# Second layer's self-attention: PSUM banks shared out anew, turns in a row, output copies one slot later, and the output product in two slots

## The chip, the cores and the metric

The kernel runs on one core of a Trainium2 chip. The metric is the device time of one execution in microseconds (us); a verdict compares medians of runs of the kernel before and of the changed kernel on the same chip.

## The reference

Two pre-norm decoder layers on x of shape (16, 256, 256): 16 batches of 256 tokens with 256 features. Each layer adds self-attention, cross-attention and a mixture of experts to x. The change concerns one of these six parts, the self-attention of the second layer:

```python
def _L1_attn_ref(x, Wq, bq, Wk, bk, Wv, bv, Wo, bo):
    h = NUM_HEADS                      # 16 heads of width 64
    q = _split_heads(x @ Wq + bq, h)   # Wq, Wk, Wv: (256, 1024)
    k = _split_heads(x @ Wk + bk, h)
    v = _split_heads(x @ Wv + bv, h)
    scale = 1.0 / jnp.sqrt(jnp.float32(ATTN_DIM))
    pattern = jnp.einsum('bhid,bhjd->bhij', k, q) * scale
    prob = jax.nn.softmax(pattern, axis=-2)
    out = jnp.einsum('bhis,bhid->bhsd', prob, v)
    return concat(out) @ Wo + bo
...
x = x + _L1_attn_ref(_layernorm(x, axis=-1), L1_attn_Wq, ...)
```

## The kernel before

x stays in SBUF throughout. The stage is `l1_attention`, from line 1235 on; it occupies the span from about 1895 to 2807 us. All four compute engines run a program of their own over the batches (`over_batches`: batches -1 to 2 written out, 3 to 14 in a loop, 15 and 16 written out), and meet at semaphores only. Each engine executes its instructions in the order written.

A batch has 16 heads, handled as 8 **pairs**, and is worked in 8 **slots** h = 0 to 7 (`batch`, one in each engine's block). Precision is kept by splitting operands into a high and a low part (`HIGH_LOW`): a product is three products (`split_product`, line 68).

For a pair, the steps are spread over several slots:

- `scores` (TensorE, line 1384): 12 products into `s_ps`, 2 banks of PSUM for the two heads of the pair.
- `maximum` (DVE, L1529), `exponents` (ACT, L1460, four instructions that also sum), in the same slot. `invert` (DVE, L1534) and `normalise` (GpSimd, L1504) one slot later.
- `turn` (TensorE, L1393): the probabilities of one head are transposed into the bank `pT_ps`, for the pair of three slots before (`TURN` = 3). `take_turned` (DVE, L1541) copies it to SBUF.
- `attend` (TensorE, L1404): the product with v into `o_ps`, for the pair of four slots before (`ATTEND` = 4). `take_out` makes its high part on ACT (L1482) and its low part on DVE (L1545), in the same slot.

Between these, each slot holds **pieces** from the table `order`, entries (kind, number, batch offset, slot). X: transposes of the normalised x of the next batch (L1416). C: the k and q of one pair (12 products). V: a quarter of v (6 products of 512 columns). W: half of the output product, on the batch before (24 products). A piece i is filled on TensorE into the bank `fill[i % 2]` and waits until the piece before it in that bank is drained (`prior_in_bank`). `drain` copies it out: for X (L1470, L1551) and C (L1473, L1555) a high part on ACT and then a low part on DVE; V (L1478) on ACT alone; W (L1565) on DVE alone, which adds it to x and after W1 makes the statistics of that batch (L254 to L261). At the end of slot 2 DVE also normalises x for the next batch (L1523).

The order of the work is thus set by hand: by the order of calls in each engine's `batch`, and by the table:

```python
order = [("C", 2, 0, 0), ("V", 0, 0, 0), ("C", 3, 0, 1), ("V", 1, 0, 1), ("C", 4, 0, 2), ("C", 5, 0, 2),
         ("C", 6, 0, 3), ("C", 7, 0, 3), ("W", 0, -1, 4), ("W", 1, -1, 4), ("V", 2, 0, 5), ("V", 3, 0, 5),
         ("X", 0, 1, 6), ("X", 1, 1, 6), ("C", 0, 1, 6), ("C", 1, 1, 7)]
```

The 8 banks of PSUM hold `s_ps` twice (4 banks), `pT_ps` (1), `o_ps` (1) and `fill` twice (2).

Of the kernel before, what the change touches and what calls it, by code (L numbers as in the profile page):

```python
# [1238 lines left out]
def l1_attention(nc, sh, Wq, bq, Wk, bk, Wv, bv, Wo, bo):  # L1239
# [10 lines left out]
    TURN, ATTEND = 3, 4  # L1250
    scale = DH ** -0.5
    with ExitStack() as ctx:
# [14 lines left out]
        with ExitStack() as prep, nc.Block() as block:  # L1267
# [105 lines left out]
        with nc.Block() as block:  # L1373

            @block.tensor
            def _(pe):
                def scores(b, h):
                    pe.wait_ge(drained["C"], done("C", h, b))
                    wait_past(pe, s_exp, PAIRS * b + h - 1)
                    for t in range(TPB):  # L1380
                        for i, (x, y) in enumerate(HIGH_LOW):
                            for n in range(2):
                                r = slice(DH * n, DH * (n + 1))
                                last = pe.matmul(s_ps[h % 2][:, n, t * SEQ:(t + 1) * SEQ], kqT[x][r, h, 1, t * P:(t + 1) * P],  # L1384
                                                 kqT[y][r, h, 0, :], start=i == 0, stop=i == len(HIGH_LOW) - 1)
                    last.then_inc(s_sc, 1)

                def turn(b, h, n):
                    pe.wait_ge(s_prob, PAIRS * b + h + 1)
                    wait_past(pe, s_pT, 2 * (PAIRS * b + h) + n)  # L1390
                    for j in range(TPB):
                        for t in range(TPB):
                            last = pe.transpose(pT_ps[:, j, t * P:(t + 1) * P], prob[:, h % RING, n, t, j * P:(j + 1) * P], sh.ident[:])  # L1393
                    last.then_inc(s_pTp, 1)

                def attend(b, h):
                    pe.wait_ge(s_pT, 2 * (PAIRS * b + h) + 2)
                    if h % (PAIRS // 2) == 0:
                        pe.wait_ge(drained["V"], per_batch["V"] * b + 2 * (h // (PAIRS // 2)) + 2)
                    wait_past(pe, s_olow, PAIRS * b + h)  # L1400
                    for j in range(TPB):
                        for n in range(2):
                            at = (2 * h + n) * DH
                            last = pe.matmul(o_ps[DH * n:DH * (n + 1), 0:SEQ], v[:, j, at:at + DH], pT[:, h % 2, n, j, :],  # L1404
                                             start=j == 0, stop=j == TPB - 1)
                    last.then_inc(s_op, 1)
# [28 lines left out]
                def batch(b):  # L1435
                    for h in range(PAIRS):
# [16 lines left out]
            def _(act):  # L1453
                def exponents(b, h):
# [3 lines left out]
                    for n in range(2):  # L1458
                        for t in range(TPB):
                            last = act.activation(prob[:, h % RING, n, t, :], s_ps[h % 2][:, n, t * SEQ:(t + 1) * SEQ], ACT.Exp,  # L1460
                                                  bias=ntop[:, h % RING, n, t:t + 1], accum_out=den[:, h % RING, n, t:t + 1])
# [18 lines left out]
                def take_out(b, h):  # L1480
                    act.wait_ge(s_op, PAIRS * b + h + 1)
                    act.copy(outT[0][:, h, :], o_ps[:, 0:SEQ]).then_inc(s_ohigh, 1)  # L1482

                def batch(b):
                    for h in range(PAIRS):
                        if live(b):
                            exponents(b, h)
                        for i, kind, number, ahead in pieces_of(h):
                            if live(b + ahead):
                                drain(i, kind, number, b + ahead)  # L1490
                        attending = lagging(b, h, ATTEND)
                        if attending:
                            take_out(*attending)
# [26 lines left out]
            def _(dve):  # L1520
# [6 lines left out]
                def maximum(b, h):  # L1527
                    dve.wait_ge(s_sc, PAIRS * b + h + 1)
                    dve.tensor_reduce(ntop[:, h % RING], s_ps[h % 2][:].rearrange("p n (t s) -> p n t s", t=TPB), AXIS.X, ALU.max,  # L1529
# [6 lines left out]
                def take_turned(b, h, n):  # L1536
# [1540 lines left out]
```

## Time and profile before

| | |
|---|---|
| median of 3 runs | 3611.78 us (3607.95 to 3613.28) |
| profiled execution | 3634.84 us |
| its span | 3633.1 us |
| mean granted TensorE clock | 0.885 of 2.4 GHz |
| PE busy over the span | 2888.5 us (80%) |
| DVE, ACT, POOL busy | 1816.4, 1211.6, 500.2 us |

The profile is of one execution. PE is TensorE's matmul, PEld its weight load, DVE VectorE, ACT ScalarE, POOL GpSimd. A timeline row is the start and length in us, the engine, the line, the operation, out<-in; in brackets the idle time of that engine before it and what ended it. A waits row says who waited for whom. A window row gives busy us of each engine (and its instructions), then the granted clock as a share of full speed (1.00 is 2.4 GHz, 0.50 is 1.2 GHz) and the DMA share.

### The profile page before, as it was taken

What the parts mean: (1) busy time and instruction counts of PE and PEld (TensorE: products, weight loads), DVE (VectorE), ACT (ScalarE), POOL (GpSimd) and SP (SyncE); (2) the same over time, 40 slices, a digit from 0 to 9 for tenths busy, and PEclk for the clock granted to TensorE, in tenths of its full rate; (3) what the DMA queues carried; (4) which work ended last, traced back from release to release, by engine and by line L of the source; (5) the groups of instructions that cost most, each with busy time, mean ns of one, the idle gap of its engine ahead of it and who ended that gap; (6) DMA issues with size and microseconds to landing.
All of it is one profiled execution on the core that took longest, in us unless ns stands there. A gap on an engine that the chain in (4) does not pass through costs nothing. (4 is left out here: it accounts for less than half of the span.)

```text
span 3633.1 us, 55877 instructions
## 1 busy us (share of the span) xinstructions
PE 2888.5 (80%) x17893; PEld 2222.8 (61%) x17894; DVE 1816.4 (50%) x4037; ACT 1211.6 (33%) x3124; POOL 500.2 (14%) x408
## 2 busy tenths in 40 slices
PE   4877699999853999999218889888887879965397
PEld 3765577777652776776116777777776856644263
DVE  4555477777342222222355556555555657745323
ACT  1330134334220112112234444445443446640021
POOL 0000000000014000000423222223222101100303
PEclk9988699999865999999659999999999889985696
DMA  7000000000133111110220000000000643314363
GB/s 269 0 0 2 0 1 0 0 0 0 35 116 131 32 35 32 32 34 32 68 79 1 1 0 0 0 0 0 0 0 9 196 123 88 87 56 158 114 182 121
DMA packets 165353, 184.96 MB, mean 51 GB/s; under 512 B 22208, under 2 KB 152464, under 8 KB 163728
## 3 DMA queue, kind: packets, MB, share of 16 engines
q1 hardware_dynamic: 136464, 144.86, 12.8%
q0 software_dynamic: 9216, 25.18, 2.2%
q10 hardware_dynamic: 19584, 13.79, 1.2%
q8 instruction: 49, 0.80, 0.1%
q14 instruction: 40, 0.33, 0.0%
HBM read 115.57 MB, written 68.19 MB: 51 GB/s over the span
## 5 line engine op out<-in xcount | busy, mean ns | idle before, releaser
L1504 POOL TENSOR_TENSOR a_prob<-a_prob,a_rden 128x1024 f32<-128x1024 f32 x128 | 242.4, 1894 | 681.6 <-DVE a_rden L1534 681.6
L1460 ACT ACTIVATE a_prob<-a_s_ps,a_ntop 128x256 f32<-128x256 f32 x512 | 235.6, 473 | 293.6 <-DVE a_ntop L1529 293.6
L2645 PE MATMUL e0x_up_ps<-e0w_upT,e0x_xgT 128*128 x576 | 263.9, 601 | 0.8 <-ACT e0x_xgT L2688 0.6
L2663 PE MATMUL e0x_y_ps<-e0w_downT,e0x_hT 128*128 x1152 | 260.5, 379 | 1.0 <-DVE e0x_hT L2704 1.0
L2663 PEld LDWEIGHTS e0x_y_ps<-e0w_downT,e0x_hT 128*128 128x128 f32 x1152 | 218.8, 190 | 61.3 <-issue 35.2
L2711 DVE COPY e0x_y<-e0x_y_ps 128x256 f32<-128x256 f32 x72 | 30.6, 425 | 438.7 <-PE e0x_y_ps L2663 438.7
L1555 DVE SCALAR_TENSOR_TENSOR a_kqT_low<-a_fill,a_kq_bias,a_kqT_high 128x256 fp32r<-128x256 f32 x256 | 109.2, 479 | 231.8 <-ACT a_kqT_high L1473 231.8
L1393 PE MATMUL a_pT_ps<-ident,a_prob 128*128 128x128 f32 x1024 | 168.1, 289 | 57.1 <-DVE a_pT L1541 56.5
L2065 ACT ACTIVATE x1a_prob<-x1a_st_ps,x1a_mask_now 128x512 f32<-128x512 f32 x256 | 162.3, 687 | 88.2 <-PE x1a_st_ps L1996 86.0
L2119 DVE TENSOR_REDUCE x1a_top<-x1a_s_ps 128x4 f32<-128x1024 f32 x128 | 155.9, 1222 | 70.0 <-PE x1a_s_ps L1980 68.3
L1541 DVE COPY a_pT<-a_pT_ps 128x512 f32<-128x512 f32 x256 | 172.0, 672 | 35.5 <-PE a_pT_ps L1393 35.4
L1393 PEld LDWEIGHTS a_pT_ps<-ident,a_prob 128*128 128x128 f32 x1024 | 119.0, 145 | 89.4 <-DVE a_pT L1541 50.7
L2645 PEld LDWEIGHTS e0x_up_ps<-e0w_upT,e0x_xgT 128*128 128x128 f32 x576 | 104.3, 191 | 106.6 <-issue 106.1
L2691 ACT ACTIVATE e0x_h<-e0x_up_ps 128x512 f32<-128x512 f32 x144 | 86.0, 597 | 244.2 <-PE e0x_up_ps L2645 244.2
L1529 DVE TENSOR_REDUCE a_ntop<-a_s_ps 128x4 f32<-128x1024 f32 x128 | 155.8, 1218 | 3.3 <-PE a_s_ps L1384 1.6
L1086 ACT ACTIVATE x0b_sq<-x0b_f 128x1024 f32<-128x1024 f32 x64 | 67.9, 1061 | 261.1 <-DVE x0b_f L1158 261.1
L2748 POOL DMA_INDIRECT e0c_ya<-sorted_results,e_slots x64 | 62.2, 972 | 623.1 <-PEq L2739 595.2
L1404 PE MATMUL a_o_ps<-a_pT,a_v 128*64 128x256 f32 x1024 | 146.1, 408 | 1.0 <-DVE a_outT_low L1545 1.0
L2688 ACT COPY e0x_xgT<-e0x_t_ps 128x256 f32<-128x256 f32 x72 | 26.8, 372 | 327.8 <-PE e0x_t_ps L2636 327.8
L68 PE MATMUL a_fill<-a_xT_high,a_wk_high 128*128 128x256 f32 x256 | 85.0, 332 | 54.5 <-DVE a_xT_low L1551 51.9
L1041 PE MATMUL x_bank<-x0b_b_sb,x0b_gT 128*128 128x256 f32 x512 | 118.6, 385 | 7.2 <-issue 3.7
L1473 ACT ACTIVATE a_kqT_high<-a_fill,a_kq_bias 128x256 fp32r<-128x256 f32 x256 | 104.7, 491 | 56.0 <-PE a_fill L68 56.0
(539 smaller groups left out, 7206.0 us busy)
## 6 DMA issues: line engine op xcount, KB each, us to landing
x_qk<-head_rows SPq DMA_DIRECT2D x384, 64.0 KB
head_rows<-x1p_rows_out SPq DMA_DIRECT2D x32, 512.0 KB, 4.0
e1w_ew<-in_L_ffn_expert_w_dram SPq DMA_DIRECT2D x8, 2048.0 KB, 17.9
sorted_tokens<-zeros SPq DMA_DIRECT2D x12, 1024.0 KB, 21.1
e1x_xg<-sorted_tokens SPq DMA_DIRECT2D x96, 128.0 KB, 2.3
sorted_results<-e1x_y ACTq DMA_DIRECT2D x96, 128.0 KB, 2.4
e0x_xg<-sorted_tokens SPq DMA_DIRECT2D x72, 128.0 KB, 2.0
sorted_results<-e0x_y SPq DMA_DIRECT2D x72, 128.0 KB, 1.7
```

The costliest lines, as they stand in the source:

```text
L1041: pe.matmul(o[:, t * DIM:(t + 1) * DIM], gT[:, h, t * P:(t + 1) * P], b_sb[:, h, :], start=h == 0, stop=False)
L1393: last = pe.transpose(pT_ps[:, j, t * P:(t + 1) * P], prob[:, h % RING, n, t, j * P:(j + 1) * P], sh.ident[:])
L1404: last = pe.matmul(o_ps[DH * n:DH * (n + 1), 0:SEQ], v[:, j, at:at + DH], pT[:, h % 2, n, j, :], start=j == 0, stop=j == TPB - 1)
L1460: last = act.activation(prob[:, h % RING, n, t, :], s_ps[h % 2][:, n, t * SEQ:(t + 1) * SEQ], ACT.Exp, bias=ntop[:, h % RING, n, t:t + 1], ...
L1504: last = pool.tensor_tensor(p, p, scale_of, ALU.mult)
L1529: dve.tensor_reduce(ntop[:, h % RING], s_ps[h % 2][:].rearrange("p n (t s) -> p n t s", t=TPB), AXIS.X, ALU.max, negate=True).then_inc(s_t ...
L1541: dve.tensor_copy(pT[:, h % 2, n], pT_ps[:]).then_inc(s_pT, 1)
L1555: last = dve.scalar_tensor_tensor(kqT[1][:, number, side, :], bank[:, side * SEQ:(side + 1) * SEQ], kq_bias[:, side, number:number + 1], k ...
L2065: last = act.activation(prob[:, c % 2, j, 2 * (h % 2):2 * (h % 2) + 2, :], st_ps[:, :, j * SEQ:(j + 1) * SEQ], ACT.Exp, bias=mask_now[:, p ...
L2119: dve.tensor_reduce(dst, s_ps[h % 2][:].rearrange("p n (t s) -> p n t s", t=TPB), AXIS.X, ALU.max).then_inc(s_max, 1)
L2645: last = pe.matmul(up_ps[half][:], xgT[:, p, k, :], upT[:, bass.ds(e, 1), k, half * 512:(half + 1) * 512].rearrange("p a d -> p (a d)"), s ...
L2663: last = pe.matmul(y_ps[p][:, 0:DIM], hT[:, p, c, :], downT[:, bass.ds(e, 1), c, :].rearrange("p a d -> p (a d)"), start=c == 0, stop=c == ...
```

## The change

The scores get one pair of banks in place of two, the turned probabilities two banks (one for each head) and the output two (by the parity of the pair). The waits on them follow. Both turns and both `take_turned` come before the pieces. Output copies run five slots after the scores (`TAKE` = 5), one after the attend, ahead of the drains; for the last pair of a batch at the very start of slot 4. W0 and W1 stand in slots 4 and 5, C5 in slot 3, C7 in slot 5, V2 and V3 with both X in slot 6, C0 in slot 7.

```diff
-    TURN, ATTEND = 3, 4
+    TURN, ATTEND, TAKE = 3, 4, 5
...
-        s_ps = [ps(f"s_ps{n}", [P, 2, 512]) for n in range(2)]
-        pT_ps = ps("pT_ps", [P, TPB, SEQ])
-        o_ps = ps("o_ps", [P, 512])
+        s_ps = ps("s_ps", [P, 2, 512])
+        pT_ps = [ps(f"pT_ps{n}", [P, TPB, SEQ]) for n in range(2)]
+        o_ps = [ps(f"o_ps{n}", [P, 512]) for n in range(2)]
...
-        order = [("C", 2, 0, 0), ("V", 0, 0, 0), ("C", 3, 0, 1), ("V", 1, 0, 1), ("C", 4, 0, 2), ("C", 5, 0, 2),
-                 ("C", 6, 0, 3), ("C", 7, 0, 3), ("W", 0, -1, 4), ("W", 1, -1, 4), ("V", 2, 0, 5), ("V", 3, 0, 5),
-                 ("X", 0, 1, 6), ("X", 1, 1, 6), ("C", 0, 1, 6), ("C", 1, 1, 7)]
+        order = [("C", 2, 0, 0), ("V", 0, 0, 0), ("C", 3, 0, 1), ("V", 1, 0, 1), ("C", 4, 0, 2), ("C", 5, 0, 3),
+                 ("C", 6, 0, 3), ("W", 0, -1, 4), ("C", 7, 0, 5), ("W", 1, -1, 5), ("V", 2, 0, 6), ("V", 3, 0, 6),
+                 ("X", 0, 1, 6), ("X", 1, 1, 6), ("C", 0, 1, 7), ("C", 1, 1, 7)]
...
                 def scores(b, h):
-                    wait_past(pe, s_exp, PAIRS * b + h - 1)
+                    wait_past(pe, s_exp, PAIRS * b + h)
...
                 def turn(b, h, n):
-                    wait_past(pe, s_pT, 2 * (PAIRS * b + h) + n)
+                    wait_past(pe, s_pT, 2 * (PAIRS * b + h) + n - 1)
...
                 def attend(b, h):
-                    wait_past(pe, s_olow, PAIRS * b + h)
+                    wait_past(pe, s_olow, PAIRS * b + h - 1)
...
                         if turning:
                             turn(*turning, 0)
+                            turn(*turning, 1)
                         for i, kind, number, ahead in pieces:
                             piece(i, kind, number, b + ahead, b)
-                        if turning:
-                            turn(*turning, 1)
...
                 def take_out(b, h):
                     act.wait_ge(s_op, PAIRS * b + h + 1)
-                    act.copy(outT[0][:, h, :], o_ps[:, 0:SEQ]).then_inc(s_ohigh, 1)
+                    if h == 0:
+                        wait_past(act, filled["W"], TPB * b)
+                    act.copy(outT[0][:, h, :], o_ps[h % 2][:, 0:SEQ]).then_inc(s_ohigh, 1)
...
+                        taking = lagging(b, h, TAKE)
+                        last_pair = taking and taking[1] == PAIRS - 1
+                        if last_pair:
+                            take_out(*taking)
                         if live(b):
                             exponents(b, h)
+                        if taking and not last_pair:
+                            take_out(*taking)
```

DVE's `batch` changes in the same way: output copy of the last pair, maximum, invert, both `take_turned`, output copy, drains. `maximum` and `exponents` read the one `s_ps`.

ACT in slots 5 and 6 before (batch 1; `a_v` is a V drain, `a_outT_high` the high part of an output; the semaphores carry the names of their first users, `n0_dve_step` is the attend's):

```order
L1460 ACTIVATE a_prob,a_den<-a_s_ps,a_ntop 128x256 [waits load_x0_loaded,load_zeroed]
L1460 ACTIVATE a_prob,a_den<-a_s_ps,a_ntop 128x256 x3
L1478 COPY a_v<-a_fill 128x512 [waits a0_pT_ready] x2
L1482 CAST a_outT_high<-a_o_ps 128x256 [waits n0_dve_step]
L1460 ACTIVATE a_prob,a_den<-a_s_ps,a_ntop 128x256 [waits load_x0_loaded,load_zeroed]
L1460 ACTIVATE a_prob,a_den<-a_s_ps,a_ntop 128x256 x3
L1470 CAST a_xT_high<-a_fill 128x256 [waits a0_x_updated] x2
```

and now, the same two slots:

```order
L1459 ACTIVATE a_prob,a_den<-a_s_ps,a_ntop 128x256 [waits load_x0_loaded,load_zeroed]
L1459 ACTIVATE a_prob,a_den<-a_s_ps,a_ntop 128x256 x3
L1483 CAST a_outT_high<-a_o_ps 128x256 [waits a0_pT_in_psum,n0_dve_step]
L1472 ACTIVATE a_kqT_high<-a_fill,a_kq_bias 128x256 [waits a0_out_in_psum]
L1472 ACTIVATE a_kqT_high<-a_fill,a_kq_bias 128x256
L1459 ACTIVATE a_prob,a_den<-a_s_ps,a_ntop 128x256 [waits load_x0_loaded,load_zeroed]
L1459 ACTIVATE a_prob,a_den<-a_s_ps,a_ntop 128x256 x3
L1483 CAST a_outT_high<-a_o_ps 128x256 [waits n0_dve_step]
L1477 COPY a_v<-a_fill 128x512 [waits a0_pT_ready] x2
L1469 CAST a_xT_high<-a_fill 128x256 [waits a0_x_updated] x2
```

The output copy has moved ahead of the drains, the first of a batch waits for `a0_pT_in_psum` too, which is the count of filled W pieces, and C7 and both V and X copies stand behind it.

DVE before, in slot 4 and the start of slot 5 (`x_resident<-x_resident,a_fill` adds a W piece, `a_ntop` is the maximum):

```order
L1541 COPY a_pT<-a_pT_ps 128x512
L1565 TENSOR_TENSOR x_resident<-x_resident,a_fill 128x256 x2
L55 MEMSET scratch 128x1
L254 BN_STATS a_parts<-x_resident 128x6 x2
L55 MEMSET scratch 128x1
L258 BN_AGGR a_means<-a_parts 128x2 x2
L261 TENSOR_SCALAR x_stats<-a_means 128x4
L1541 COPY a_pT<-a_pT_ps 128x512
L1545 TENSOR_TENSOR a_outT_low<-a_o_ps,a_outT_high 128x256
L1529 TENSOR_REDUCE a_ntop<-a_s_ps 128x4
```

and now, slot 5 and the start of slot 6:

```order
L1533 TENSOR_REDUCE a_ntop<-a_s_ps 128x4
L1538 RECIPROCAL a_rden<-a_den 128x4
L1545 COPY a_pT<-a_pT_ps 128x512 x2
L1549 TENSOR_TENSOR a_outT_low<-a_o_ps,a_outT_high 128x256
L1559 SCALAR_TENSOR_TENSOR a_kqT_low<-a_fill,a_kq_bias,a_kqT_high 128x256 x2
L1569 TENSOR_TENSOR x_resident<-x_resident,a_fill 128x256
L55 MEMSET scratch 128x1
L254 BN_STATS a_parts<-x_resident 128x6 x2
L55 MEMSET scratch 128x1
L258 BN_AGGR a_means<-a_parts 128x2 x2
L261 TENSOR_SCALAR x_stats<-a_means 128x4
L1533 TENSOR_REDUCE a_ntop<-a_s_ps 128x4
```

W1's addition and the statistics stood behind W0's and ahead of a turned copy; they stand behind C7's low part and directly ahead of slot 6's maximum.

TensorE now, from the last product of V3 in slot 6 to the first of C0 in slot 7 (before, `L1416 MATMUL a_fill<-ident,a_xn`, the X pieces, was followed at once by that C0 product):

```order
L68 MATMUL a_fill<-a_wv_high,a_xT_low 128x512
L1416 MATMUL a_fill<-ident,a_xn 128x128 x4
L1404 MATMUL a_o_ps<-a_pT,a_v 64x256 x4
L1384 MATMUL a_s_ps<-a_kqT_high 128x256 x2
L1384 MATMUL a_s_ps<-a_kqT_low,a_kqT_high 128x256 x2
L1384 MATMUL a_s_ps<-a_kqT_high,a_kqT_low 128x256 x2
L1384 MATMUL a_s_ps<-a_kqT_high 128x256 x2
L1384 MATMUL a_s_ps<-a_kqT_low,a_kqT_high 128x256 x2
L1384 MATMUL a_s_ps<-a_kqT_high,a_kqT_low 128x256 x2
L1393 MATMUL a_pT_ps<-ident,a_prob 128x128 x8
L68 MATMUL a_fill<-a_xT_high,a_wk_high 128x256
```

Attend, scores and two turns have come between X and C0.

## Rows read from the trace of the kernel before

**Rows 1.** Busy time by engine in batches 1 to 14: window, length, engines, clock, DMA

```profile
1950.38:2734.76 784.38, 692.25 (x5547) 566.93 (x5546) 454.81 (x966) 372.26 (x1317) 229.34 (x126) 0.96 0.00 0
```

**Rows 2.** Waits of PE, same stretch: us in total, times, longest

```profile
PE a_fill L68 <- DVE a_xT_low L1551: 47.5, 14, 3.4
PE a_pT_ps L1393 <- DVE a_pT L1541: 44.2, 54, 1.3
```

**Rows 3.** Timeline of PE: W0 to the next turn, then one C and V slot

```profile
2201.81 0.36 PE L68 MATMUL a_fill<-a_wo_high,a_outT_high 128*128 128x256 f32 x1
...
2207.56 0.60 PE L1393 MATMUL a_pT_ps<-ident,a_prob 128*128 128x128 f32 x4
...
2236.66 0.38 PE L1384 MATMUL a_s_ps<-a_kqT_high 64*128 64x256 f32 x2
...
2237.98 0.37 PE L68 MATMUL a_fill<-a_xT_high,a_wk_high 128*128 128x256 f32 x1
...
2239.50 0.39 PE L68 MATMUL a_fill<-a_wv_high,a_xT_high 128*128 128x512 f32 x1
...
2240.89 0.60 PE L1393 MATMUL a_pT_ps<-ident,a_prob 128*128 128x128 f32 x4
2241.42 1.08 PE L1404 MATMUL a_o_ps<-a_pT,a_v 128*64 128x256 f32 x8
2242.43 0.39 PE L1384 MATMUL a_s_ps<-a_kqT_high 64*128 64x256 f32 x2
```

**Rows 4.** Timeline of PE: slot 6 and the start of slot 7

```profile
2215.23 0.39 PE L1384 MATMUL a_s_ps<-a_kqT_high 64*128 64x256 f32 x2
...
2220.62 0.38 PE L68 MATMUL a_fill<-a_xT_high,a_wk_high 128*128 128x256 f32 x1 [3.39 <-DVE a_xT_low L1551]
...
2225.21 0.39 PE L1384 MATMUL a_s_ps<-a_kqT_high 64*128 64x256 f32 x2
```

**Rows 5.** Windows of one microsecond inside that slot's C piece

```profile
2222.00:2223.00 1.00, 1.00 (x7) 1.00 (x5) 0.00 (x0) 0.00 (x0) 0.00 (x0) 0.50 0.00 0
```

**Rows 6.** Timeline of ACT: V copies, a slot with one C, C copies of two

```profile
2213.72 1.08 ACT L1478 COPY a_v<-a_fill 128x512 f32<-128x512 f32 x2
...
2227.56 0.47 ACT L1460 ACTIVATE a_prob<-a_s_ps,a_ntop 128x256 f32<-128x256 f32 x1 [1.86 <-DVE a_ntop L1529]
...
2229.37 0.85 ACT L1473 ACTIVATE a_kqT_high<-a_fill,a_kq_bias 128x256 fp32r<-128x256 f32 x2
2230.08 0.40 ACT L1482 CAST a_outT_high<-a_o_ps 128x256 fp32r<-128x256 f32 x1
...
2246.60 1.58 ACT L1473 ACTIVATE a_kqT_high<-a_fill,a_kq_bias 128x256 fp32r<-128x256 f32 x4
```

**Rows 7.** Timeline of DVE: the same slot, and slot 2's normalisation

```profile
2226.22 1.22 DVE L1529 TENSOR_REDUCE a_ntop<-a_s_ps 128x4 f32<-128x1024 f32 x1
...
2230.25 0.88 DVE L1555 SCALAR_TENSOR_TENSOR a_kqT_low<-a_fill,a_kq_bias,a_kqT_high 128x256 fp32r<-128x256 f32 x2 [2.15 <-ACT a_kqT_high L1473]
2231.04 0.68 DVE L1541 COPY a_pT<-a_pT_ps 128x512 f32<-128x512 f32 x1
...
2231.97 1.22 DVE L1529 TENSOR_REDUCE a_ntop<-a_s_ps 128x4 f32<-128x1024 f32 x1
...
2249.99 0.73 DVE L1523 TENSOR_SCALAR a_xn<-x_resident,x_stats,x_rstd 128x256 f32 x2
```

**Rows 8.** Timeline of DVE: W1 added, statistics, next instruction

```profile
2263.48 0.42 DVE L1565 TENSOR_TENSOR x_resident<-x_resident,a_fill 128x256 f32 x1 [2.31 <-PE a_fill L68]
...
2265.25 0.69 DVE L1541 COPY a_pT<-a_pT_ps 128x512 f32<-128x512 f32 x1
```

**Rows 9.** First layer: waits of PE, 60 to 260 us, and two windows

```profile
PE a_wt L437 <- DVE a_xn L551: 33.9, 15, 2.6
...
129.00:131.00 2.00, 2.00 (x6) 1.55 (x6) 0.00 (x0) 0.50 (x1) 0.00 (x0) 0.50 0.00 0
179.00:181.00 2.00, 2.00 (x11) 1.77 (x10) 0.00 (x0) 0.91 (x3) 0.00 (x0) 1.00 0.00 0
```

More of the change, by code:

```diff
@@ L1383, in scores @@
                                 r = slice(DH * n, DH * (n + 1))
-                                last = pe.matmul(s_ps[h % 2][:, n, t * SEQ:(t + 1) * SEQ], kqT[x][r, h, 1, t * P:(t + 1) * P],
+                                last = pe.matmul(s_ps[:, n, t * SEQ:(t + 1) * SEQ], kqT[x][r, h, 1, t * P:(t + 1) * P],
                                                  kqT[y][r, h, 0, :], start=i == 0, stop=i == len(HIGH_LOW) - 1)
@@ L1389, in turn @@
                     pe.wait_ge(s_prob, PAIRS * b + h + 1)
-                    wait_past(pe, s_pT, 2 * (PAIRS * b + h) + n)
+                    wait_past(pe, s_pT, 2 * (PAIRS * b + h) + n - 1)
                     for j in range(TPB):
                         for t in range(TPB):
-                            last = pe.transpose(pT_ps[:, j, t * P:(t + 1) * P], prob[:, h % RING, n, t, j * P:(j + 1) * P], sh.ident[:])
+                            last = pe.transpose(pT_ps[n][:, j, t * P:(t + 1) * P], prob[:, h % RING, n, t, j * P:(j + 1) * P], sh.ident[:])
                     last.then_inc(s_pTp, 1)
@@ L1403, in attend @@
                             at = (2 * h + n) * DH
-                            last = pe.matmul(o_ps[DH * n:DH * (n + 1), 0:SEQ], v[:, j, at:at + DH], pT[:, h % 2, n, j, :],
+                            last = pe.matmul(o_ps[h % 2][DH * n:DH * (n + 1), 0:SEQ], v[:, j, at:at + DH], pT[:, h % 2, n, j, :],
                                              start=j == 0, stop=j == TPB - 1)
@@ L1459, in exponents @@
                         for t in range(TPB):
-                            last = act.activation(prob[:, h % RING, n, t, :], s_ps[h % 2][:, n, t * SEQ:(t + 1) * SEQ], ACT.Exp,
+                            last = act.activation(prob[:, h % RING, n, t, :], s_ps[:, n, t * SEQ:(t + 1) * SEQ], ACT.Exp,
                                                   bias=ntop[:, h % RING, n, t:t + 1], accum_out=den[:, h % RING, n, t:t + 1])
@@ L1528, in maximum @@
                     dve.wait_ge(s_sc, PAIRS * b + h + 1)
-                    dve.tensor_reduce(ntop[:, h % RING], s_ps[h % 2][:].rearrange("p n (t s) -> p n t s", t=TPB), AXIS.X, ALU.max,
+                    dve.tensor_reduce(ntop[:, h % RING], s_ps[:].rearrange("p n (t s) -> p n t s", t=TPB), AXIS.X, ALU.max,
                                       negate=True).then_inc(s_top, 1)
@@ L1540, in take_turned @@
                         wait_past(dve, s_op, g - 1)
-                    dve.tensor_copy(pT[:, h % 2, n], pT_ps[:]).then_inc(s_pT, 1)
+                    dve.tensor_copy(pT[:, h % 2, n], pT_ps[n][:]).then_inc(s_pT, 1)
                 def take_out(b, h):
                     dve.wait_ge(s_ohigh, PAIRS * b + h + 1)
-                    dve.tensor_tensor(outT[1][:, h, :], o_ps[:, 0:SEQ], outT[0][:, h, :], ALU.subtract).then_inc(s_olow, 1)
+                    dve.tensor_tensor(outT[1][:, h, :], o_ps[h % 2][:, 0:SEQ], outT[0][:, h, :], ALU.subtract).then_inc(s_olow, 1)
                 def drain(i, kind, number, own):
@@ L1573, in batch @@
                     for h in range(PAIRS):
-                        turning, attending = lagging(b, h, TURN), lagging(b, h, ATTEND)
+                        turning, taking = lagging(b, h, TURN), lagging(b, h, TAKE)
+                        last_pair = taking and taking[1] == PAIRS - 1
+                        if last_pair:
+                            take_out(*taking)
                         if live(b):
@@ L1581, in batch @@
                             take_turned(*turning, 0)
+                            take_turned(*turning, 1)
+                        if taking and not last_pair:
+                            take_out(*taking)
                         for i, kind, number, ahead in pieces_of(h):
```

7 lines of the change are left out of this document (removed).

## The prediction

> **What bounds the kernel now.** The change touches one stage, the second layer's self-attention, so I read that stage alone. First the busy times over its fourteen full batches, 1 to 14, from the scores of one batch to those of another [rows 1]: 784.38 us, 56.03 a batch, in which TensorE is busy 692.25 us (88%), DVE 454.81, ACT 372.26. TensorE is the bound, and the reader should ask what its other 12% are. The waits view gives them by name [rows 2]: 47.5 us in 14 waits for the low part of the turned x, 44.2 us in 54 waits for the copy of the turned probabilities, together 6.55 us a batch.
>
> A batch is eight slots, one head pair each. The timeline of a slot without a wait gives the prices on TensorE [rows 3]: scores and first turn 1.32 us (2236.66 to 2237.98), a C piece 1.52, a V piece 1.39, the second turn 0.53, the attend 1.01, in all 5.77; two W pieces take 5.75 between them, 2.87 each. Slot 6 holds the long wait [rows 4]: 9.98 us, with 3.39 before the C piece. Then the granted clock is 0.50, that is 1.2 GHz [rows 5], after TensorE had stood still for those 3.39 us. At full clock the slot would be 1.32 + 0.5 for the two X pieces + 3.39 + 1.65 + 0.53 + 1.01 = 8.4 to 8.6, so the low clock costs 1.4 us here; other batches show slots of 11.0, and over the fourteen I put it at 1.8. What is left, 56.03 - 6.55 - 1.8 = 47.7, is TensorE's own work in a batch.
>
> Last, why those waits exist, from ACT and DVE. After a maximum the exponents start 1.34 us later (2226.22, 2227.56) and hold ACT 1.81 us, then the high part of a C piece 0.85, then DVE's low part 0.79, the second turned copy and the output's low part, and only then the next maximum at 2231.97 [rows 6, 7]. So maximum follows maximum every 5.75 us, a chain as long as TensorE's slot; with two C pieces (1.58 on ACT [rows 6], 1.58 on DVE) it is longer than the slot and TensorE waits at the turn.
>
> **The change, part by part.** No arithmetic is added or removed: 47.7 us of TensorE work stay. With both turns in a row, the second no longer follows another kind of product: 0.42 (as the first turn, part of the 1.32) instead of 0.53 would give 8 x 0.11 = 0.9 back; nothing is the other end. I take 0.5, in the middle, since the attend now follows a piece instead: 47.2.
>
> *Removed: the waits for the turned copy*, 44.2/14 = 3.2 us a batch. Two banks, and copies that stand ahead of the drains in DVE's queue. The chain also loses the second copy (about 0.60, 2231.04 on) and the output's low part (0.33), and gains the output's high part ahead of the drains on ACT (0.3): 5.75 - 0.93 + 0.3 = 5.1 for a C slot. TensorE's 5.8 covers it.
>
> *Removed in part: the wait for x*, 3.39. Between X and C0 now stand attend, scores and two turns, 1.01 + 1.32 + 0.42 = 2.75 us, and C0 begins slot 7's pieces. But X moves behind V2 and V3 in slot 6, and waits for their copies out of the same two banks.
>
> *One pair of score banks*: scores wait for the exponents of the pair before. From scores to maximum 1.01 (2225.21, 2226.22), to exponents 1.34, to their end about 1.95: 4.35 us with the hop. Only slot 2, with the single piece C4 (5.77 - 1.39 = 4.38), is as short. Price 0 to 0.1; taken 0.05.
>
> *Slots 3 and 4.* In slot 2 DVE still normalises (0.65 [rows 7]) before the maximum of slot 3, which comes at 2.35 + 1.81 + 0.3 + 0.85 + 0.79 + 0.65 = 6.75 after slot 2's scores, 2.4 after slot 3's. Its exponents start at 3.7, its two C pieces leave DVE at 3.7 + 1.81 + 0.3 + 0.85 + 1.58 + hops = 8.3, and the last pair's output has its low part at 8.7. Slot 4 starts at 5.85; W0 is ready to go at 1.8 in it and waits until 2.9: **1.1 us**, where a turn waited before.
>
> *Slot 5 is where I expect the gain to leak.* Output copies now run in the slot after their attend. For pair 0 that is slot 5, and ACT must first wait until W1 of the batch before is filled, since it overwrites what W1 reads. W1 is TensorE's last piece there: it ends at 1.8 + 1.5 + 2.87 + 0.15 = 6.3 in the slot. Behind that wait on ACT stands C7's high part, behind C7 on DVE stand the W1 addition and the statistics (1.77 from addition to next instruction [rows 8]), and behind those the maximum of slot 6. Worked out: output copy 6.35, C7 high 6.65 to 7.5, C7 low to 8.3, W1 and statistics to 10.05. Slot 6 starts at 7.25, so its maximum comes 2.8 into it instead of 1.0. Exponents from 4.15 to 5.95 in slot 6, output copy to 6.25, the two V copies (1.08 for two [rows 6]) leave bank 0 at 6.85 and bank 1 at 7.3. TensorE is ready for X0 at 1.8 + 2.78 = 4.6: it waits **2.3 us**, and 0.2 more between X0 and X1. The x wait has not gone; it is 2.5 us instead of 3.39.
>
> *Slot 7.* C0 is no longer a slot ahead of the scores that read it: 2.35 + 1.81 + 0.3 + 0.85 + 0.9 = 6.25 from slot 7's start against a slot of 5.85: **0.4 us**. Waits in all: 0.05 + 1.1 + 2.5 + 0.4 = 4.05.
>
> *The clock.* The nearest rows for a 2.3 us wait are in the first layer's attention: TensorE waits there 15 times, up to 2.6 us [rows 9]. Of the fourteen of 1.8 to 2.6 us, seven were followed by a granted clock of 0.50 within 3 us (such as 129 to 131) and seven were not (179 to 181). Here a second short wait follows at once, so I take six in ten, at 1.8 each: 1.1. Ends: 0, and 2.4 (a slot of 11.0 less 8.6) each time.
>
> **Sum.** 47.2 + 4.05 + 1.1 = 52.35 a batch, 3.7 less than 56.03; fourteen batches give 52. Batch 0 has no W, so its ACT never waits in slot 5; it loses nearly the whole x wait and its low clock: 5. In batch 15 the turn waits go (3.2) and W0's comes (1.1), slot 6 is late: 2. Together 59 us. The profiled execution took 3634.84 us around a span of 3633.1; it would take 3576. It lies 23 us above the median of the timed runs, 3611.78, and I take the same saving from that: **3553**.
>
> The Trainium skill ("TensorE: Matmul & The Clock Gate", on HAM oscillation) reports a kernel in which PSUM double buffering, added once TensorE was kept fed, gave no further gain. By that rule this sum would be zero. The row of 44.2 us of waits for one PSUM bank speaks against it here.
>
> **Rivals.**
> *The wait in slot 5 is hidden, and so the x wait is gone.* For it: ACT is idle half the time. Against: its queue is in order, and the wait is for TensorE's last piece. It would give 47.2 + 1.55 = 48.75, 7.3 a batch, with the ends 111 us: 3501.
> *More waits than I count.* Every slot is now within 0.7 us of the ACT and DVE chain, and each hop that I round down comes on top; with 0.15 us a slot and the low clock in each batch, 1.2 + 1.3 more a batch: 35 us, 3588. Against: the prices are start to start, hops included.
> *Slower: the clock.* A low clock after the 2.3 us wait, and also after W0's 1.1 and C0's 0.4, at the 2.4 of a long drop each, is 7.2 a batch: 47.2 + 4.05 + 7.2 = 58.45, 2.4 more than before; less the 7 of batches 0 and 15, 27 us slower: 3639. It decides from 4.8 us of clock loss a batch on. Against: 54 turn waits of up to 1.3 us stand in the trace, and the mean clock of the stage is 0.96 [rows 1, 2], which slot 6 uses up by itself.
> The Trainium skill (same page, its second failure mode, cycling through PSUM banks) says that short pauses between groups can make the clock go back and forth; that is this rival. The turn waits of the trace do not show it.
> *The change doing nothing* can be left out: the order of instructions shows the turns in a row, and the banks are named in the rows.
>
> **Numbers.** Forecast 0.62 (its own range 3530 to 3575); hidden wait 0.12; more waits 0.18; clock 0.04; the stage unchanged within the error 0.04. About 0.2% is what a measurement of this kernel can tell from no change, 7 us. The range goes from 3520, between the hidden wait and the forecast, to 3592, just past the case of more waits; outside lie the hidden wait, the slower clock and no change, two in ten. Faster 0.92, same 0.04, slower 0.04.
>
> **What would show it.** Right: waits for the turned copy nearly gone; a wait of 1 to 1.2 us at W0 for the output's low part; ACT's output copy of slot 5 idle about 2 us with W1 as releaser; X0 waiting some 2.3 us for a V copy; a batch of 51.5 to 53. Wrong: an x wait under 0.5 us, a batch under 50 or over 55, a granted clock under 0.94 over the stage, or waits of scores for exponents in more slots than slot 2.

## The result, and the profile after

The change takes 3525.44 us (median of 4 runs, 3524.37 to 3530.47) against 3609.88 us for the kernel before on the same chip: the ratio is 0.9768, 95% interval 0.9751 to 0.9785, 84 us less. 3553 was predicted, with a range of 3520 to 3592.

The two profiled executions differ by more, 3634.84 against 3530.47. Of these 104 us the stage makes 80: from its first C piece to the first scores of the stage behind it, 1034.0 us (1896.3 to 2930.3) became 953.8 (1877.1 to 2830.9). 19 us of the rest lie ahead of the stage, in the first layer's experts and behind them, where the kernels do not differ: TensorE's last wait ahead of the stage, for one, is 122.4 us for 134.0. They are no part of what the change does.

First the view of [rows 1] and [rows 2] for the changed kernel, over the same fourteen batches. The first fence has window, length, busy us of PE, PEld, DVE, ACT and POOL, and the granted clock. The second has who waited for whom, total, times and longest.

```profile
1926.64:2645.43 718.79, 672.07 (x5544) 548.03 (x5545) 463.40 (x967) 367.21 (x1316) 229.53 (x126) 0.99 0.00 0
```

```profile
PE a_fill L1416 <- ACT a_v L1477: 28.8, 14, 2.1
ACT a_outT_high L1483 <- PE a_fill L68: 28.6, 14, 2.2
...
PE a_fill L68 <- DVE a_outT_low L1549: 13.0, 14, 1.0
...
PE a_s_ps L1384 <- DVE a_kqT_low L1559: 4.7, 13, 0.4
```

718.79 us are 51.34 a batch, where 56.03 stood. TensorE is busy 93% of them in place of 88%. The waits for the turned copy are gone, and so is the wait ahead of C0. Three waits of TensorE take their place: X0 for the V copy (2.1 us each), W0 for the output's low part (0.93), and the scores for C0's low part (0.36). ACT has a new one of its own, for W1 (2.0), which answers to none of before.

The eight slots, in us from the start of one slot's scores to that of the next, read from the timeline of TensorE. After: a batch in which the granted clock stayed at 1.00. Before: one of the batches in which it was low for the shorter of the two times seen (in every batch of before it fell to 0.50 at slot 6).

| slot | 0 | 1 | 2 | 3 | 4 | 5 | 6 | 7 | batch |
|---|---|---|---|---|---|---|---|---|---|
| before | 6.91 | 5.77 | 5.82 | 6.45 | 9.99 | 6.13 | 9.98 | 4.55 | 55.6 |
| after | 5.77 | 5.76 | 4.43 | 5.81 | 6.97 | 7.20 | 8.70 | 6.25 | 50.9 |

The place on which the prediction rested most, slots 5 and 6. TensorE (answers to [rows 4]): scores of slot 5, of slot 6, X0, scores of slot 7.

```profile
2264.03 0.39 PE L1384 MATMUL a_s_ps<-a_kqT_high 64*128 64x256 f32 x2
...
2271.23 0.39 PE L1384 MATMUL a_s_ps<-a_kqT_high 64*128 64x256 f32 x2
...
2278.14 0.85 PE L1416 MATMUL a_fill<-ident,a_xn 128*128 128x128 f32 x4 [2.09 <-ACT a_v L1477]
...
2279.94 0.39 PE L1384 MATMUL a_s_ps<-a_kqT_high 64*128 64x256 f32 x2
```

ACT in the same stretch (answers to [rows 6]): the output copy that waits for W1, C7's high part, the first exponent of slot 6, the V copies.

```profile
2270.33 0.37 ACT L1483 CAST a_outT_high<-a_o_ps 128x256 fp32r<-128x256 f32 x1 [2.01 <-PE a_fill L68]
2270.59 0.84 ACT L1472 ACTIVATE a_kqT_high<-a_fill,a_kq_bias 128x256 fp32r<-128x256 f32 x2
2275.33 0.47 ACT L1459 ACTIVATE a_prob<-a_s_ps,a_ntop 128x256 f32<-128x256 f32 x1 [3.89 <-DVE a_ntop L1533]
...
2277.40 1.10 ACT L1477 COPY a_v<-a_fill 128x512 f32<-128x512 f32 x2
```

DVE (answers to [rows 8]): C7's low part, the addition of W1, the maximum of slot 6.

```profile
2271.47 0.88 DVE L1559 SCALAR_TENSOR_TENSOR a_kqT_low<-a_fill,a_kq_bias,a_kqT_high 128x256 fp32r<-128x256 f32 x2 [0.32 <-ACT a_kqT_high L1472]
2272.26 0.41 DVE L1569 TENSOR_TENSOR x_resident<-x_resident,a_fill 128x256 f32 x1
...
2274.00 1.22 DVE L1533 TENSOR_REDUCE a_ntop<-a_s_ps 128x4 f32<-128x1024 f32 x1
```

Read in order: ACT stands 2.01 us until W1 is filled (2270.33, 6.3 us into slot 5), C7's low part follows at 2271.47, W1 and its statistics, and the maximum at 2274.00, 2.77 us into slot 6 in place of 1.0. The exponents hold ACT to 2277.1, the V copies come then, and X0 starts at 2278.14, 2.09 us late.

### The profile page after: what moved, and what is told of

It reads as the page before. It is cut to its first block and busy times, and to the rows that moved or that the text cites. A ratio compares the mean times of both kernels' runs of the same rounds, so it can differ in the third digit from the quotient of the medians.

```text
span 3528.7 us, 55915 instructions
## 1 busy us (share of the span) xinstructions
PE 2860.3 (81%) x17893; PEld 2200.3 (62%) x17894; DVE 1824.1 (52%) x4037; ACT 1206.1 (34%) x3124; POOL 501.0 (14%) x408
## 5 line engine op out<-in xcount | busy, mean ns | idle before, releaser
L1545 DVE COPY a_pT<-a_pT_ps 128x512 f32<-128x512 f32 x256 | 160.9, 669 | 0.7 <-PE a_pT_ps L1393 0.7
L1393 PE MATMUL a_pT_ps<-ident,a_prob 128*128 128x128 f32 x1024 | 140.9, 281 | 0.0
L1549 DVE TENSOR_TENSOR a_outT_low<-a_o_ps,a_outT_high 128x256 fp32r<-128x256 f32 x128 | 54.1, 423 | 148.6 <-ACT a_outT_high L1483 148.6
L1393 PEld LDWEIGHTS a_pT_ps<-ident,a_prob 128*128 128x128 f32 x1024 | 110.3, 142 | 18.4 <-issue 1.8
L2916 PE MATMUL e1x_y_ps<-e1w_ew,e1x_xgT 128*128 x384 | 109.3, 407 | 8.3 <-DVE e1x_y L2950 4.3
```

The source lines that it names most:

```text
L1393: last = pe.transpose(pT_ps[n][:, j, t * P:(t + 1) * P], prob[:, h % RING, n, t, j * P:(j + 1) * P], sh.ident[:])
L1545: dve.tensor_copy(pT[:, h % 2, n], pT_ps[n][:]).then_inc(s_pT, 1)
```

## Experiments

All are edits of the changed kernel. They ran on several chips, on which the kernel before took 3609 to 3633 us, so each is given by its distance to the kernel before of the same chip (the change: -84 us, and -80 when it was run again), and by the profile's us per batch over batches 1 to 14 (the change: 51.3). Differences of 4 us between such distances are within their intervals. What an edit loses or gains is its worth with all the rest of the change in place; these worths overlap and do not add up to 84.

### The table of before

```diff
-                 ("C", 6, 0, 3), ("W", 0, -1, 4), ("C", 7, 0, 5), ("W", 1, -1, 5), ("V", 2, 0, 6), ("V", 3, 0, 6),
-                 ("X", 0, 1, 6), ("X", 1, 1, 6), ("C", 0, 1, 7), ("C", 1, 1, 7)]
+                 ("C", 6, 0, 3), ("C", 7, 0, 3), ("W", 0, -1, 4), ("W", 1, -1, 4), ("V", 2, 0, 5), ("V", 3, 0, 5),
+                 ("X", 0, 1, 6), ("X", 1, 1, 6), ("C", 0, 1, 6), ("C", 1, 1, 7)]
```

(and C5 in slot 2 again.)

> The changed kernel with the table of pieces of the kernel before (W0 and W1 in slot 4, V2 and V3 in slot 5, C0 in slot 6). Theory (the banks, the turns in a row and the later output copies bring most of the gain, the table about 1 us a batch): W1 is filled before slot 5, so ACT does not wait for it; the wait ahead of C0 is back at about 3.5 us, and the granted clock falls after it in every batch; the turn waits stay away. Worked out from the rows 52.4 us a batch, 1.1 more than the change, so about 3540 us. Rival (the table did the main part by taking C0 away from X): near the kernel before, 55 us a batch or more, 3575 us or more.

Measured: 3575.08 against 3632.99 us, ratio 0.9842 (0.9825 to 0.9858), -58 us; 52.9 us a batch. Of its waits over batches 1 to 14 (who for whom, us in total, times, longest):

```profile
PE a_fill L68 <- DVE a_xT_low L1555: 46.1, 14, 3.3
...
PE a_fill L68 <- DVE a_outT_low L1549: 4.6, 14, 0.4
```

The wait ahead of C0 is back (46.1 us in 14), no ACT wait for W1 exists, and slot 6 takes 9.7 to 10.5 us with the clock falling in each batch. So the table is worth 26 us of the 84, more than the 15 expected (1.5 us a batch for 1.1, and batch 0, 3.3 us longer, was not counted), and 58 us come with the old table too. The rival, 55 us a batch or more, falls.

### The turns apart

```diff
                         if turning:
                             turn(*turning, 0)
-                            turn(*turning, 1)
                         for i, kind, number, ahead in pieces:
                             piece(i, kind, number, b + ahead, b)
+                        if turning:
+                            turn(*turning, 1)
```

and on DVE `take_turned(*turning, 1)` behind the drains in the same way.

> The changed kernel with the second turn after the pieces again, and its copy on DVE after the drains; both banks for the turned probabilities stay. Theory (what the order buys is that the copy of 0.6 us leaves the chain from drains to the next maximum): slots 0 and 1 unchanged at 5.8, the maxima of slots 3, 4 and 6 later by 0.6 to 1.2, slot 3 at 6.3, the W0 wait 1.6, the x wait 2.7: 53.1 us a batch, 3550 us. Rival (the second bank alone removed the waits, the order is worth nothing): 51.3 us a batch, 3525 us.

Measured: 3608.59 against 3632.99 us, ratio 0.9936 (0.9920 to 0.9953), -24 us; 54.8 us a batch.

Of its waits over batches 1 to 14 (who for whom, us in total, times, longest):

```profile
PE a_fill L1416 <- ACT a_v L1478: 37.8, 14, 2.7
...
PE a_fill L68 <- DVE a_outT_low L1550: 28.9, 14, 2.1
...
PE a_s_ps L1384 <- ACT a_prob L1460: 6.0, 14, 0.4
```

Slots 0 and 1 are unchanged (5.79, 5.77), slot 3 takes 6.33 and X0 waits 2.7, as expected, and no wait for a turned copy comes back: the second bank alone keeps those away. W0 waits 2.1 us where 1.6 was expected, and slot 6 takes 10.7 us, 1.4 more than its wait explains: after 2.5 to 2.7 us of standing the clock fell in fourteen batches of fourteen, which the expectation had left out. The order of turns and copies is worth 60 us of the 84, in later waits (W0, X0) and in the clock, and the rival, that it is worth nothing, falls.

### One bank for the turned probabilities

```diff
-        pT_ps = [ps(f"pT_ps{n}", [P, TPB, SEQ]) for n in range(2)]
+        pT_ps = [ps("pT_ps", [P, TPB, SEQ])] * 2
...
-                    wait_past(pe, s_pT, 2 * (PAIRS * b + h) + n - 1)
+                    wait_past(pe, s_pT, 2 * (PAIRS * b + h) + n)
```

> The changed kernel with one bank for the turned probabilities, both turns still in a row. Theory (the second bank and the order carry each other: in a row on one bank, the second turn waits until DVE, after its maximum, has copied the first): the second turn starts at 2.95 us into a slot in place of 1.3, 1.6 us more in each slot and 3.4 in slot 6 where the maximum is late; the waits at W0, X0 and C0 go. 61.8 us a batch, 5.8 more than the kernel before, about 80 us slower than it. Rival (the order alone is good, the bank a detail): within 20 us of the change.

Measured: 3740.09 against 3608.72 us, ratio 1.0368 (1.0351 to 1.0385), 131 us slower than the kernel before; 64.3 us a batch.

Of its waits over batches 1 to 14 (who for whom, us in total, times, longest):

```profile
PE a_pT_ps L1393 <- DVE a_pT L1545: 188.0, 112, 3.1
```

112 waits, 188 us: the second turn of each slot. The slots are 7.4, 7.4, 6.0, 7.8, 7.5, 8.8, 11.8, 7.4; slot 6, where the second turn waits 3.1 us and the clock falls in twelve batches of fourteen, is most of what the expectation missed; in four batches it falls in slot 3 as well. Bank and order carry each other: the order on one bank is far slower than the kernel before, and two banks without the order leave 24 us of the gain of 84.

### One output bank

```diff
-        o_ps = [ps(f"o_ps{n}", [P, 512]) for n in range(2)]
+        o_ps = [ps("o_ps", [P, 512])] * 2
...
-                    wait_past(pe, s_olow, PAIRS * b + h - 1)
+                    wait_past(pe, s_olow, PAIRS * b + h)
```

> The changed kernel with one output bank in place of two, the attend waiting for the output copy of the pair just before. Theory (an output's low part is finished about 5.05 us into the slot, the attend starts at 4.8 in a slot of 5.8, at 3.4 in slot 2, at 6.2 in slot 5, where the copy comes 7.2 in): waits of 0.3 us in slots 0, 1 and 3, 1.7 in slot 2 and 1.0 in slot 5; W0's wait goes and the x wait falls to about 1.1. In all 1.5 us a batch more: 52.9 without loss of clock, 22 us slower than the change, 62 below the kernel before. Rival (the copy is early enough, the second output bank is idle): the change's 84 below.

Measured: 3587.40 against 3631.38 us, ratio 0.9876 (0.9859 to 0.9893), -44 us; 52.7 us a batch.

Of its waits over batches 1 to 14 (who for whom, us in total, times, longest):

```profile
PE a_o_ps L1404 <- DVE a_outT_low L1549: 54.3, 82, 1.7
...
PE a_fill L1416 <- ACT a_v L1477: 13.5, 14, 1.0
```

The batch is near what was worked out (52.7 for 52.9), the attend waits in 82 places and the x wait falls to 1.0. The second output bank is worth 40 us, half of them in the fourteen batches. The other half lies in batch 15 and behind it: 206 us from its first scores to the next stage's, against 185. Of these 21 us, 4 are in its slots and 14 between its last scores and the first W product (26.3 us for 12.7), where TensorE works at 1.2 GHz: the granted clock is 0.50 there, and an attend takes 1.97 us for 1.08. The first attend behind the last scores:

```profile
2736.32 1.97 PE L1404 MATMUL a_o_ps<-a_pT,a_v 128*64 128x256 f32 x8 [3.07 <-DVE a_outT_low L1549]
```

So of those 14 us about half are waits for the output copies (8.7 in all for 2.2 in the change), and the other half is the clock. It also fell in two of the fourteen batches, both times after the attend's wait of 1.7 us in slot 2.

### Pair 0's output copy behind the drains

```diff
-                        if taking and not last_pair:
+                        first_pair = taking and taking[1] == 0
+                        if taking and not last_pair and not first_pair:
                             take_out(*taking)
                         for i, kind, number, ahead in pieces_of(h):
                             if live(b + ahead):
                                 drain(i, kind, number, b + ahead)
+                        if first_pair:
+                            take_out(*taking)
```

on ACT and on DVE.

> The changed kernel with the output copy of pair 0 (ACT and DVE, slot 5) behind the drains of its slot in place of ahead of them. Theory (ACT's wait for W1 holds C7, the statistics and so slot 6's maximum): ACT takes C7 at once, the maximum of slot 6 starts about 1.2 us into the slot in place of 2.8, the x wait falls from 2.1 to 0.7 us, the clock stays at 1.00: 49.4 us a batch, 27 us less than the change, 3498 us. Rival (the V copies behind the exponents make the x wait by themselves): x wait over 1.8 us, 3520 us or more.

Measured: 3523.91 against 3632.99 us, ratio 0.9698 (0.9682 to 0.9714), -109 us; 49.4 us a batch.

Its busy times over batches 1 to 14, the granted clock third from the end:

```profile
1946.24:2637.16 690.92, 664.98 (x5546) 544.08 (x5546) 463.49 (x967) 366.96 (x1316) 229.56 (x126) 1.00 0.00 0
```

and its waits there:

```profile
PE a_fill L68 <- DVE a_outT_low L1552: 13.1, 14, 1.0
...
PE a_fill L1416 <- ACT a_v L1477: 7.7, 14, 0.6
```

ACT still waits for W1, 1.3 us, but no drain of the slot stands behind it. The maximum of slot 6 starts 1.28 us into the slot, the x wait is 0.6 us, the clock 1.00. Expectation and measurement agree to 0.1 us a batch, and the rival (the V copies make the wait by themselves) falls.

### W1 ahead of C7

```diff
-                 ("C", 6, 0, 3), ("W", 0, -1, 4), ("C", 7, 0, 5), ("W", 1, -1, 5), ("V", 2, 0, 6), ("V", 3, 0, 6),
+                 ("C", 6, 0, 3), ("W", 0, -1, 4), ("W", 1, -1, 5), ("C", 7, 0, 5), ("V", 2, 0, 6), ("V", 3, 0, 6),
```

> The changed kernel with W1 ahead of C7 in slot 5; the output copies stay where the change put them. Theory (ACT is held until W1 is filled, so an earlier W1 frees it earlier): ACT waits until 4.8 us into the slot in place of 6.3, the statistics run ahead of C7's low part, slot 6's maximum starts at 1.0 to 1.1, the x wait is 0.5 us, the clock stays at 1.00: 49.3 us a batch, 109 to 111 below the kernel before, as with pair 0's copy moved behind. Rival (it was the copy's place ahead of the drains, not the wait for W1, that cost): x wait over 1.5 us, 84 to 90 below.

Measured: 3519.12 against 3631.38 us, ratio 0.9686 (0.9669 to 0.9703), -112 us; 49.2 us a batch.

Of its waits over batches 1 to 14 (who for whom, us in total, times, longest):

```profile
ACT a_outT_high L1483 <- PE a_fill L68: 8.5, 14, 0.7
...
PE a_fill L1416 <- ACT a_v L1477: 4.7, 14, 0.4
```

A second way to the same end: ACT's wait shrinks to 0.6 us, the x wait to 0.3, and slot 6's maximum starts 1.02 us in. The rival, that the copy's place alone cost, falls. It was the wait for W1 in front of C7's copy: moving the output copy behind or W1 ahead removes it alike.

### The normalisation in slot 4

```diff
-                        if h == 2 and live(b) and live(b + 1):
+                        if h == 4 and live(b) and live(b + 1):
                             dve.wait_ge(filled["X"], per_batch["X"] * (b + 1))
                             normalise(b + 1)
```

> The changed kernel with the normalisation of the next batch's x at the end of DVE's slot 4 in place of slot 2. Theory (the 0.65 us of it on DVE are what makes slot 3's and slot 4's maximum and the last pair's output late): the W0 wait falls from 0.95 to 0.3 us, 0.65 us a batch, 9 us in all, 3516 us. Rival (the two C pieces of slot 3 alone make W0 wait): W0 wait over 0.8, 3525 us; or the 0.65 come back as a later maximum in slot 5: 3525 us with no W0 wait.

Measured: 3548.71 against 3632.99 us, ratio 0.9769 (0.9753 to 0.9786), -84 us, the same as the change; 51.3 us a batch.

Its busy times over batches 1 to 14, the granted clock third from the end:

```profile
1939.06:2657.10 718.04, 681.42 (x5545) 554.73 (x5546) 464.28 (x967) 368.35 (x1316) 229.67 (x126) 0.97 0.00 0
```

and its waits there:

```profile
PE a_fill L1416 <- ACT a_v L1477: 28.9, 14, 2.1
...
PE a_fill L68 <- DVE a_outT_low L1549: 4.1, 14, 0.3
```

W0's wait fell from 13.0 to 4.1 us in all, as expected, and a batch in which the clock holds takes 50.3 in place of 50.9. But the clock, 0.99 over the fourteen batches in the change, is 0.97: after the same x wait it fell in eleven batches of fourteen, not in five. Neither the theory nor a rival had this. The second rival's time came out, but not its reason: slot 5 is 7.21 us, as in the change.

### Both edits

Pair 0's output copy behind the drains, and the normalisation in slot 4.

> The two edits of the runs before together: pair 0's output copy behind the drains of slot 5, and the normalisation in DVE's slot 4. Alone the normalisation's move shortened slot 4 by 0.64 us but gained nothing in all, because the granted clock fell after the x wait of 2.1 us in eleven batches of fourteen in place of five. Theory (the gain was real and the clock took it back; with a short x wait it stays): 49.43 - 0.64 = 48.8 us a batch, clock 1.00, 9 us less than with pair 0's edit alone: 118 us below the kernel before. Rival (the normalisation only moves the lateness elsewhere): same time as with pair 0's edit alone, 109 below.

Measured: 3517.31 against 3631.38 us, ratio 0.9685 (0.9666 to 0.9704), -114 us; 48.7 us a batch, with a granted clock of 1.00.

Its busy times over batches 1 to 14:

```profile
1945.55:2627.70 682.15, 665.25 (x5545) 544.30 (x5546) 463.76 (x967) 366.94 (x1316) 229.53 (x126) 1.00 0.00 0
```

With the x wait at 0.6 us the clock holds and the 0.6 us a batch are kept, by the profile: 48.82 against 49.43 in the batches of the loop. The timed runs are less sharp: -114 against -109, and the two intervals overlap.

### Three output copies behind

Pairs 0, 1 and 2 behind the drains (`taking[1] < 3`), and the normalisation in slot 4.

> As the run with both edits, and the output copies of pairs 1 and 2 (slots 6 and 7) behind the drains as well. Theory: the V copies and C0's high part each start 0.26 us earlier on ACT, so the x wait is 0.3 us in place of 0.55 and the wait ahead of the next batch's scores 0.1 in place of 0.37: 48.3 us a batch, 125 below the kernel before. Rival (the output's low part then delays the next maximum on DVE by 0.33 us): no gain, 118 below, with slot 0 or 7 longer.

Measured: 3507.51 against 3631.38 us, ratio 0.9655 (0.9638 to 0.9673), -124 us; 48.2 us a batch. This is the fastest version found; 40 us further below the kernel before than the change.

Its busy times over batches 1 to 14, the granted clock third from the end:

```profile
1942.76:2617.55 674.79, 664.81 (x5544) 543.95 (x5545) 460.64 (x967) 367.85 (x1317) 229.78 (x126) 1.00 0.00 0
```

and its waits there:

```profile
PE a_fill L1416 <- ACT a_v L1477: 4.6, 14, 0.3
...
PE a_fill L68 <- DVE a_outT_low L1552: 4.1, 14, 0.3
```

TensorE is busy 98.5% of the fourteen batches. What is left to it of named waits is 0.6 us a batch. Against the run with both edits, on the same chip, it wins 10 us; its four executions (3502 to 3509 us) all lie below the four of that run (3513 to 3522), and the profile shows 0.5 us a batch less.

### The change again

> The change itself once more, on the chip of these runs. Expected: 84 us below the kernel before, eight slots of 5.77, 5.77, 4.43, 5.81, 6.97, 7.21, 8.70 and 6.26 us where the clock holds, the x wait 2.1 us in every batch. Open: in how many of the fourteen batches the granted clock falls after it; it was five, and eleven with the normalisation moved. If it is a property of the wait's length alone the count should be near five again.

Measured: 3528.26 against 3608.72 us, ratio 0.9774 (0.9758 to 0.9791), -80 us; 51.3 us a batch, the same slots to 0.02 us, the x wait 28.9 us in 14. The clock fell in four batches of fourteen, near the five of the first time.

## Why the prediction came out as it did

**What bounds the kernel** was right: TensorE's own work, 47.7 us a batch before, is 47.3 after (50.9 less the waits of 3.65 in the table below). With its named waits taken down to 0.6 the best version comes to 48.2 us a batch, so no further wait of size came to light behind them.

**The turn waits** (3.2 us a batch) went, as put, and the chain on ACT and DVE stayed inside TensorE's slot: slots 0, 1 and 3 are 5.77, 5.76 and 5.81 where 5.8 was worked out. With one bank they come back in every slot. With the turns apart they do not: the bank is what removes them, and what the order adds is that the second copy no longer makes the later maxima late (slot 3 takes 6.33 us without it, W0 and X0 wait longer).

**The waits that come**, term by term:

| | predicted | measured |
|---|---|---|
| W0 for the last pair's low part | 1.1 | 0.93 |
| X0 for V's copy, and X1 | 2.3 + 0.2 | 2.1 + 0.25 (the row of the X pieces is 0.85 us long, 0.60 where they follow each other) |
| scores for C0 | 0.4 | 0.36 |
| scores for the exponents, slot 2 | 0.05 | slot 2 is 4.43, 4.38 worked out |
| TensorE's own work | 47.2 | 47.3 |
| low clock | 1.1 | 0.44 |
| batch | 52.35 | 51.34 |

**Slot 5 as the leak** was right in its place, its order of events and nearly its size: W1 filled 6.3 us in (6.3 worked out), maximum of slot 6 2.77 in (2.8). Two separate edits that free C7's copy from the wait bring 25 and 28 us more.

**Too small was the gain: 59 us for 84.** By the profile the stage won 80.3, in two parts; the other 4 are not in the stage of these two executions, and the change run again gave 80 in all. Over the fourteen batches 65.7 against 52: the term that was mis-sized most is the clock, taken from the first layer as six falls in ten at 1.8 us each where it was 5 and 4 in fourteen at 1.4 each (0.44 us a batch for 1.1), and the waits were 0.4 us a batch too long. The ends gave 14.6 against 7. From batch 15's first scores to the next stage 195.5 us became 185.5, where the prediction had 2: its slots gave 3.6 of these 10, and 5.0 came between the last scores and the first W product. The prediction's "in batch 15 ... 2" stopped at the slots and left out what runs after the last scores, where only turns and attends remain and nothing covers a turn wait. The timeline of TensorE behind the last scores, before: four second turns and the first W product.

```profile
2782.58 0.63 PE L1393 MATMUL a_pT_ps<-ident,a_prob 128*128 128x128 f32 x4 [1.49 <-DVE a_pT L1541]
...
2785.91 0.63 PE L1393 MATMUL a_pT_ps<-ident,a_prob 128*128 128x128 f32 x4 [1.10 <-DVE a_pT L1541]
...
2789.17 0.63 PE L1393 MATMUL a_pT_ps<-ident,a_prob 128*128 128x128 f32 x4 [1.03 <-DVE a_pT L1541]
...
2792.43 0.63 PE L1393 MATMUL a_pT_ps<-ident,a_prob 128*128 128x128 f32 x4 [1.03 <-DVE a_pT L1541]
...
2797.19 0.36 PE L68 MATMUL a_fill<-a_wo_high,a_outT_high 128*128 128x256 f32 x1 [1.01 <-DVE a_outT_low L1545]
```

The same after: both turns of a pair, an attend, and the first W product.

```profile
2689.64 1.22 PE L1393 MATMUL a_pT_ps<-ident,a_prob 128*128 128x128 f32 x8
2691.66 1.08 PE L1404 MATMUL a_o_ps<-a_pT,a_v 128*64 128x256 f32 x8 [0.80 <-DVE a_outT_low L1549]
...
2699.27 0.36 PE L68 MATMUL a_fill<-a_wo_high,a_outT_high 128*128 128x256 f32 x1 [1.01 <-DVE a_outT_low L1549]
```

The last scores start at 2779.54 and 2686.59, so W starts 17.7 us behind them before and 12.7 after: the four turn waits, 4.65 us, are most of it.

Batch 0 gave 4.9 us where 5 was put, and that is in part luck. Its x wait did go (3.4 us became 0.2), but 3.8 us of turn waits went too, which the prediction did not name, and the single pair of score banks cost four waits for the exponents, 5.6 us, the longest this one:

```profile
1907.66 0.38 PE L1384 MATMUL a_s_ps<-a_kqT_high 64*128 64x256 f32 x2 [2.50 <-ACT a_prob L1459]
```

So the price of 0 to 0.1 us for that bank holds in batches 1 to 14, whose slots are longer, and not in batch 0.

**Rivals.** That the wait of slot 5 is hidden (3501) did not happen, but the runs that remove it land at that distance from the kernel before: -109 and -112 for the 111 worked out. That the totals agree so well is in part luck: their batches take 49.4 and 49.2 us where 48.75 was worked out, and the ends gave more. More waits than counted did not come: slots 0, 1 and 3 hold none. The slower rival, clock falls after each of three waits a batch, did not happen: in both executions of the change falls followed only the x wait, never W0's 0.93 us or the scores' 0.36. The Trainium skill ("TensorE: Matmul & The Clock Gate", second failure mode) says of another kernel that short pauses between groups made the clock go back and forth; here the falls came after the one long pause of a batch and after none of the short ones. The same page's report (on HAM oscillation) that PSUM double buffering gave another kernel no further gain does not carry over to this one, where the second turn bank decides between 84 us gained and 131 lost.

**Range and chances.** The time lies in the range, near its lower end, and 5 us below the forecast's own range: the clock and the waits were counted too high, and the end of the stage too low. Of the signs named ahead, one was missed by little: a batch of 51.34 us where 51.5 to 53 stood.

Two parts of the change were never taken out by themselves: the single pair of score banks, and the output copies one slot later. What each of them is worth stays open.

## What to carry to other kernels

Ask of each new wait what stands behind it in the queue of the waiting engine: an output copy of 0.37 us that waited 2 us for a product cost 25 to 28 us in all, because a drain, the statistics and a maximum stood behind it; a few lines further down it cost almost nothing. Here a second bank paid in full only with an order that fills both in a row (24 us of the 84 without it), and the order only with the bank (131 us lost without it). And price the first batch and the run-out after the last one apart: a wait that is covered in the loop can be bare there.

## What was not expected of the hardware

How often the granted clock falls after a stand of TensorE is not a matter of its length alone. Counted over batches 1 to 14 of each profile, falls against stands:

| stand of TensorE | where | falls |
|---|---|---|
| 3.4 us | kernel before, ahead of C0 | 14 of 14 |
| 3.3 | old table, ahead of C0 | 14 of 14 |
| 2.5 to 2.7 | turns apart, ahead of X0 | 14 of 14 |
| 3.1 | one turn bank, slot 6 | 12 of 14 |
| 2.1 | change, ahead of X0, two executions | 3 and 2 of 12 |
| 2.1 | normalisation in slot 4, ahead of X0 | 9 of 12 |
| 2.1 | turns apart, ahead of W0 | 2 of 14 |
| 1.9 | the same three as for 2.1 ahead of X0, batches 1 and 2 | 6 of 6 |
| 1.8 to 1.9 | one turn bank, slot 3 | 4 of 14 |
| 1.6 to 1.7 | one output bank, slot 2 | 2 of 14 |
| under 1.6 | all twelve profiles | none of some 500 |

The row of 1.9 us is the plainest: in the two batches that are written out ahead of the loop X0 waits a little less, and there the clock fell every time (and so it did ahead of W0 with the turns apart, in these two batches alone). The first in the change:

```profile
1969.11 0.93 PE L1416 MATMUL a_fill<-ident,a_xn 128*128 128x128 f32 x4 [1.86 <-ACT a_v L1477]
```

A fall costs about 1.4 us of a batch in the change (52.3 for 50.9). Two stretches behind the same x wait of the change, one without a fall and one with (window, length, busy us, granted clock):

```profile
2279.00:2282.00 3.00, 3.00 (x30) 2.33 (x31) 1.89 (x3) 0.37 (x1) 0.00 (x0) 1.00 0.00 0
2381.00:2384.00 3.00, 3.00 (x21) 1.75 (x20) 0.85 (x2) 0.50 (x2) 0.00 (x0) 0.59 0.00 0
```

What decides among stands of 1.6 to 2.1 us was not tried and stays open. An edit elsewhere can lose its gain this way, as the normalisation's did (0.63 us a batch won in the slots, none in the total) until the wait itself was short.
